# Swin block on one core: who zeroes the values buffers, and where the bias product stands

## What is computed

```python
xn = ln2d(x, norm1_g, norm1_b)                  # over the 64 channels
windows = partition(roll(xn, (-4, -4)), 8)      # 64 windows of 64 tokens
q, k, v = split(windows @ in_w.T + in_b)        # 8 heads of 8 channels
attn = softmax(q @ k.T / sqrt(8)) @ v
y = x + roll(reverse((attn @ out_w.T + out_b) @ proj_w.T + proj_b), (4, 4))
z = ln2d(y, norm2_g, norm2_b)
return y + (gelu(z @ fc1_w.T + fc1_b) @ fc2_w.T + fc2_b)
```

## Time and profile before

| | before |
|---|---|
| median of 3 runs | 90.39 us (90.39 to 90.66) |
| time of the profiled execution | 90.42 us |
| span of the profiled execution | 88.6 us |
| granted TensorE clock, mean | 1.0 |
| busy share: TensorE, VectorE, ScalarE, GpSimd | 93%, 73%, 56%, 47% |

### The profile page before, as it was taken

How to read it: one execution, slowest core, us unless ns; L and a number is a source line. 1 busy time by engine, 2 the same in 40 slices (tenths; PEclk the granted TensorE clock), 3 DMA queues, 4 the chain that set the end, 5 groups by cost and what they waited for, 6 DMA issues and landing times.

```text
span 88.6 us, 4248 instructions
## 1 busy us (share of the span) xinstructions
PE 82.6 (93%) x1794; PEld 51.9 (59%) x1794; DVE 65.0 (73%) x188; ACT 50.1 (56%) x83; POOL 41.7 (47%) x52
## 2 busy tenths in 40 slices
PE   5997999799999999999999999989999999999950
PEld 5974846466775676586686567646664453233420
DVE  4999989898999799669869698999760854333160
ACT  0395998853678296396396156334469486453500
POOL 7988819988108516940930930340717135800000
PEclk9999999999999999999999999999999999999999
DMA  1799400111111111010111110000000000030233
GB/s 23 222 351 424 182 29 0 63 44 52 44 51 37 59 49 51 31 65 31 51 37 59 45 50 24 4 0 11 7 0 7 0 0 0 7 118 37 81 141 100
DMA packets 3619, 5.74 MB, mean 65 GB/s; under 512 B 1072, under 2 KB 1840, under 8 KB 3472
## 3 DMA queue, kind: packets, MB, share of 16 engines
q1 hardware_dynamic: 2736, 3.08, 10.1%
q10 hardware_dynamic: 864, 2.38, 7.1%
HBM read 2.64 MB, written 1.05 MB: 42 GB/s over the span
## 4 chain that ended last, share of the span: by engine, by line
PE 83%; DVE 7%; DMA 3%; issue 2%; ACT 1%; SPq 1%
PE ps_s L310 17%; PE ps_u L392 10%; PE ps_t L375 8%; PE ps_u L467 5%; PE ps_m L285 5%; PE ps_o L408 4%; PE ps_t L310 4%; PE ps_s L451 4%; PE ps_t L451 3%; PE ps_o L420 3%; DMA masked<-qk 3%; PE ps_m L274 2%; PE ps_m L451 2%; PE ps_m L375 2%; PE ps_o L467 2%; PE ps_m L297 2%
## 5 line engine op out<-in xcount | busy, mean ns | idle before, releaser
L883 ACT ACTIVATE probs<-ps_t 128x1024 f32<-128x1024 f32 x13 | 13.3, 1024 | 13.3 <-PE ps_t L375 13.2
L627 DVE TENSOR_REDUCE row_max<-ps_s 128x16 f32<-128x1024 f32 x15 | 18.3, 1219 | 3.1 <-PE ps_s L310 2.4
L310 PE MATMUL ps_s<-masked,qk 32*64 32x256 f32 x240 | 16.8, 387 | 1.1 <-DMA masked<-qk 0.5
L1016 POOL TENSOR_TENSOR rstd<-y_var,minus_half 128x4 f32<-128x4 f32 x8 | 8.2, 1031 | 15.5 <-DVE y_var L681 15.5
L310 PE MATMUL ps_t<-masked,qk 32*64 32x256 f32 x224 | 15.5, 388 | 0.0
L310 PEld LDWEIGHTS ps_s<-masked,qk 32*64 32x64 f32 x240 | 8.4, 131 | 3.9 <-issue 1.4
L392 PE MATMUL ps_u<-probs,vz 128*32 128x64 f32 x512 | 10.5, 222 | 0.0
L392 PEld LDWEIGHTS ps_u<-probs,vz 128*32 128x32 f32 x512 | 7.9, 110 | 4.4 <-issue 4.2
L375 PE MATMUL ps_t<-max_x,minus_sel 128*128 128x512 f32 x26 | 9.4, 443 | 0.0
L992 POOL TENSOR_TENSOR rstd<-var,minus_half 128x4 f32<-128x4 f32 x8 | 8.6, 1070 | 1.0 <-DVE var L615 0.4
L641 DVE STREAM_TRANSPOSE sums<-ps_u 128x512 f32<-128x512 f32 x8 | 5.7, 710 | 4.5 <-PE ps_u L392 4.5
(11 more groups left out here) (110 smaller groups left out, 153.8 us busy)
## 6 DMA issues: line engine op xcount, KB each, us to landing
masked<-qk SPq DMA_DIRECT2D x54, 32.0 KB, 2.1
x_ch<-x_ch_d ACTq DMA_DIRECT2D x1, 1024.0 KB, 8.5
out_d<-result SPq DMA_DIRECT2D x3, 256.0 KB, 2.5
x_tok<-x_tok_d ACTq DMA_DIRECT2D x1, 512.0 KB, 6.4
late<-late_d ACTq DMA_DIRECT2D x1, 352.0 KB, 5.1
x_tok<-x_tok_d SPq DMA_DIRECT2D x2, 128.0 KB, 3.4
x_tok<-x_tok_d ACTq DMA_DIRECT2D x1, 256.0 KB, 4.5
out_d<-result SPq DMA_DIRECT2D x2, 128.0 KB, 2.2
```

Source lines behind the costliest of these rows:

```text
L310: return nc.tensor.matmul(ps[L * u:L * u + L, g, n * TOK:(n + 1) * TOK], qk[r:r + RG, b, w, t], masked[r:r + RG, b, :, w, t], start=(n == ...
L627: nc.vector.tensor_reduce(row_max[:, 16 * w:16 * w + 16], score_bank(k, w)[:].rearrange("q g (h j) -> q (g h) j", j=L), axis=AX.X, op=ALU. ...
L883: nc.scalar.activation(probs[:, w, :], scores_t_bank(k, w)[:].rearrange("q g c -> q (g c)"), ACT.Exp).then_inc(probs_done, 1)
L1016: nc.gpsimd.tensor_tensor(rstd2[:].rearrange("q n w -> q (n w)"), y_var[:].rearrange("q n w -> q (n w)"), minus_half[:], op=ALU.pow).then_ ...
```

## The change

VectorE no longer zeroes `vz` 1. ScalarE zeroes buffer 1 in place of 2 and 3, and GpSimd zeroes 0, 2, 3 and 4. On GpSimd the scaling of tile 2 now waits until VectorE has finished the six masks of tile 0 (`k_masked_dve` at 2), and the scaling of tile 3 until VectorE has masked tile 1 (`k_masked_dve` at 3); `zero_masked(3)`, which waited for the first maxima, now follows the scaling of tile 3. On TensorE the bias product moves from behind the first eight warm-up products to behind `x_transpose(0)`, and of the fourteen warm-up products ahead of the first projection thirteen are left, in another division. The thresholds of the waits for zeroed buffers follow.

```diff
--- before.py
+++ after.py
@@ -137,7 +137,6 @@
         masked_zeroed = [sem(f"masked_zeroed{i}") for i in range(QB)]
         vz_zeroed = sem("vz_zeroed")
         vz_zeroed_act = sem("vz_zeroed_act")
-        vz_zeroed_dve = sem("vz_zeroed_dve")
         vz_set = sem("vz_set")
         bias_product_done = sem("bias_product_done")
         b_qk_made = sem("b_qk_made")
@@ -547,16 +546,16 @@
             pe.wait_ge(zeros_set, 1)
             warm_up(8)
             pe.wait_ge(early_loaded, 16)
-            nc.tensor.matmul(ps_o[:, 0, 0:1], w_in_t[0:C, 0:2 * C], vec[0:C, B1:B1 + 1],
-                             start=True, stop=True).then_inc(bias_product_done, 1)
-            warm_up(3)
+            warm_up(2)
             pe.wait_ge(mean_w_set, 1)
             pe.wait_ge(w_in_scaled, 1)
             nc.tensor.matmul(ps_u[:, 0, 0:3 * C], mean_w[:], w_scaled[:],
                              start=True, stop=True).then_inc(w_in_mean_done, 1)
+            warm_up(2)
+            x_transpose(0)
+            nc.tensor.matmul(ps_o[:, 0, 0:1], w_in_t[0:C, 0:2 * C], vec[0:C, B1:B1 + 1],
+                             start=True, stop=True).then_inc(bias_product_done, 1)
             warm_up(1)
-            x_transpose(0)
-            warm_up(2)
             pe.wait_ge(w_qkv_made, 1)
             project_qk(0)
             late_products_out()
@@ -775,7 +774,7 @@
                     spread_max_dve(t + 1)
                 if t == 0:
                     late_weights()
-                    dve.wait_ge(vz_zeroed, 2)
+                    dve.wait_ge(vz_zeroed, 4)
                     set_ones(VB - 1, VB)
                 if tile_ok(t - 1):
                     scale_attn(t - 1)
@@ -786,7 +785,6 @@
             nc.vector.memset(zeros[:], 0.0).then_inc(zeros_set, 1)
             nc.vector.memset(mean_w[:], 1.0 / P).then_inc(mean_w_set, 1)
             nc.vector.memset(masked[:, 0].rearrange("q h w t -> q (h w t)"), 0.0).then_inc(masked_zeroed[0], 1)
-            nc.vector.memset(vz[:, 1].rearrange("q w n h e -> q (w n h e)"), 0.0).then_inc(vz_zeroed_dve, 1)
             ln1_stats(0)
             ln1_var_first()
             dve.wait_ge(early_loaded, 16)
@@ -812,9 +810,8 @@
             spread_max_dve(0)
             mask_k_half(1)
             ln1_stats(4)
-            dve.wait_ge(vz_zeroed, 1)
-            dve.wait_ge(vz_zeroed_dve, 1)
-            dve.wait_ge(vz_zeroed_act, 2)
+            dve.wait_ge(vz_zeroed, 3)
+            dve.wait_ge(vz_zeroed_act, 1)
             set_ones(0, VB - 1)
             ln1_stats(5)
             for t in range(TILES):
@@ -861,13 +858,11 @@
 
             def copy_v(k):
                 act.wait_ge(v_projected, k + 1)
-                if k in (0, VB - 1):
-                    act.wait_ge(vz_zeroed, 2 if k else 1)
-                elif k == 1:
-                    act.wait_ge(vz_zeroed_dve, 1)
+                if k == 1:
+                    act.wait_ge(vz_zeroed_act, 1)
                 elif k < VB:
-                    act.wait_ge(vz_zeroed_act, k - 1)
-                if k >= VB:
+                    act.wait_ge(vz_zeroed, max(k, 1))
+                else:
                     act.wait_ge(values_weighed, 2 * (k - VB) + 2)
                 for u in range(2):
                     r = slice(L * u, L * u + L)
@@ -940,9 +935,8 @@
             nc.scalar.activation(minus_sel[:].rearrange("q a u j -> q (a u) j"), sel8.unsqueeze(2).to_broadcast([P, 8, L]),
                                  ACT.Copy).then_inc(minus_sel_made, 1)
             act.wait_ge(zeros_set, 1)
-            for b in (2, 3):
-                nc.scalar.activation(vz[:, b].rearrange("q w n h e -> q (w n h e)"), zeros[:, 0:1].to_broadcast([P, 1024]),
-                                     ACT.Copy).then_inc(vz_zeroed_act, 1)
+            nc.scalar.activation(vz[:, 1].rearrange("q w n h e -> q (w n h e)"), zeros[:, 0:1].to_broadcast([P, 1024]),
+                                 ACT.Copy).then_inc(vz_zeroed_act, 1)
             copy_xn(0)
             copy_qk_first()
             mask_k_first()
@@ -1048,16 +1042,18 @@
             ln1_rstd(0)
             ln1_rstd(1)
             ln1_scale(1)
-            pool.wait_ge(early_loaded, 16)
             ln1_rstd(2)
+            pool.wait_ge(k_masked_dve, 2)
             ln1_scale(2)
-            pool.wait_ge(max_found, 1)
+            zero_values(2)
+            zero_values(3)
+            ln1_rstd(3)
+            pool.wait_ge(k_masked_dve, 3)
+            ln1_scale(3)
             zero_masked(3)
-            ln1_rstd(3)
-            ln1_scale(3)
-            zero_values(VB - 1)
             ln1_rstd(4)
             ln1_scale(4)
+            zero_values(4)
             for t in range(TILES):
                 slot(t)
             for k in range(TILES - 3, TILES):
```

## The result

The changed kernel takes 90.84 us, the median of 20 runs; the kernel before takes 90.09 us on the same chip (20 runs). The ratio is 1.0051, with a 95% interval of 1.0029 to 1.0072: slower by some 0.46 us. The profiled execution took 90.77 us with a span of 89.0 us (before: 90.42 and 88.6). One thing has to be known to read the numbers: four of the 20 runs of the changed kernel took 92.7 to 94.3 us at a lower granted clock and are in the median but not in the ratio; the first and the sixth experiment are about them. The other sixteen fall into two groups of eight, at 90.07 to 90.47 us and at 90.77 to 91.19 us, with 90.62 us as the median of all sixteen. The profiled execution is one of the slower group.

A forecast was written before the change was run, and what follows sets the result against it. After the prologue TensorE's products bound the kernel, with VectorE's gapless list holding the hand-over. A later `b_qk` adds 0.33 us, less 0.07 of slack: 90.42 + 0.26 = 90.68 us, range 90.1 to 91.1.

The forecast's parts named there:

- The sum: Whole kernel: +0.33 us on VectorE up to the first maxima, 0.07 taken off in all, giving +0.26 us.
- rival 3: Tile 2: GpSimd, later by its waits, stalls VectorE's masks with the scaling of tile 4; 90.8 to 91.2 us, chance 0.2.
- The base: Start of the forecast: the profiled execution's 90.42 us, taken as 0.03 us above the median of the runs.
- The slack: VectorE between first maxima and tile 1's maxima: idle gaps of 0.19 and 0.07 us; only 0.07 taken off.
- The memset off VectorE: Prologue: without the 0.91 us memset of `vz` 1, `xhat` of tile 0 comes 0.31 us sooner, at 6.38.
- the load of tile 1: VectorE's statistics of tile 1: the load landing at about 5.3 limits the memset's gain to 0.31 to 0.38 us.
- `b_qk`: VectorE, tile 0: waits for the moved bias product, starts at 7.57 to 7.73, taken as +0.33 us, delaying masks and scores.
- rival 1: Tile 0: the early 0.31 us get through if `b_qk` starts before 7.30; 90.1 us, chance 0.13.
- GpSimd's wait for tile 0: Tile 0's masks: the wait removes a 0.37 us stall already covered by the first scores; worth nothing on the path.
- GpSimd's lateness: GpSimd's queued work: costed at nothing; under the slower rival, scaling of tile 4 at about 20.2 meets masks at 20.33.

The follow-up runs named there:

- experiment 1: Changed kernel with the bias product first again, in TensorE's order of before: 90.57 us, ratio 0.9991.
- sixth experiment: Changed kernel with GpSimd's scaling of tile 4 behind VectorE's masks of tile 2, and without two warm-up products before the first projection of v: 94.37 us.
- experiments 4: Kernel before with only the bias product moved behind the transposes of tile 0: 90.77 us, ratio 1.006.
- experiment 2: Changed kernel with GpSimd's scaling of tile 4 also waiting for VectorE's masks of tile 2: 90.45 us, ratio 1.0022.
- experiment 8: Changed kernel, bias product first, tile 4's scaling behind tile 2's masks; also `vz` 0 memset and statistics of tiles 1 and 3 moved later: 90.06 us, ratio 1.0014.
- Experiments 2 and 3: 3 is the changed kernel with both edits, bias product first and tile 4's scaling behind tile 2's masks: 89.81 us, ratio 0.9947; 2 has only the latter.
- experiment 7: Kernel before with GpSimd's scaling of tile 2 waiting for VectorE's six masks of tile 0: 89.97 us, ratio 0.9994.
- execution of 90.05 us: Unchanged changed kernel, one of three further profiles; it is free of the long stall of tile 2's masks: 90.05 us.

## Why the prediction was right

- **The sum.** +0.26 us was forecast, with 90.68 us and ends from +0.07 to +0.43; the ratio gives +0.46 us. The sum describes the executions without the stall: there TensorE's scores of tile 2 are 0.19 us late. In the other half rival 3 came true as well, and they are 0.95 us late. The measured average mixes the two, so it is in part luck that it lies near the sum.
- **The base.** 90.42 us was the time of one execution, which loses 0.4 us at 50 us, and the median of 20 runs is 90.09. From there the sum gives 90.35 us, against 90.62 measured at full clock. The 90.68 us came close because the base was 0.33 us too high and the stall was not in the sum.
- **The slack.** 0.07 us was taken off between the first maxima and those of tile 1. The delay shrank there from 0.38 us (11.95 against 11.57) to 0.21 (19.03 against 18.82): 0.17 us.
- **The memset off VectorE.** `xhat` was put at 6.38 and came at 6.44, and the -0.31 is -0.34 to -0.41 between experiments 4 and 2, within the noise. The reason was only half right. It was not the load of tile 1: VectorE waited for tile 0's own load until 3.73, and for GpSimd's power for the last 0.20 us. And the variance (L614) took 0.42 us, ending at 5.21 where GpSimd's memset of `vz` 0 ended at 5.19; without that memset beside it, it took 0.17 (experiment 8), as it did before, behind the memset's end.
- **`b_qk`** was put at 7.57 to 7.73 and came at 7.70; the idle gap before it, put at 0.6, was 0.57. Masks at 9.76 (9.84), first scores at 10.75 (10.79), first maxima at 11.9 (11.95), maxima of tile 1 at 19.1 (19.03): the line of work was the right one. Experiments 2 and 3 show that `b_qk` has little slack (of 0.67 us some 0.5 get through), and rival 1 was right in its condition: with `b_qk` at 7.04 the early 0.25 us get through.
- **GpSimd's wait for tile 0.** Costed at nothing, and experiment 7 gives a ratio of 0.9994.
- **GpSimd's lateness.** Scaling of tile 4 at about 20.2 and masks at 20.33 were forecast, 20.34 and 20.27 came. The step that was mis-sized is the price of their meeting: "by the fifth mask of tile 0 this costs 0.37 us, and at most the whole 0.62". The scaling cost 0.35 us, as the row said, and was swallowed, but behind it on GpSimd stood a memset of 0.95 us, which the change had moved there from behind the scaling of tile 3, and the mask waited for that too: 1.24 us in all (2.13 against 0.89). And rival 3 counted slack where there is none: it let the maxima at 21.33 be late against the scores at 26.07, but TensorE's scores at 22.78 follow them with 0.22 us between, so what is left after the 0.38 us of idle time reaches TensorE at once. I had looked for what stands behind the waiting instruction on its own engine, and not for what stands behind the one that holds it up.
- The rule of the Trainium skill that I set beside it (SBUF — State Buffer, Who interferes with whom: the pair of ports is an exclusive lock for a whole instruction, and the other fully blocks) agrees in kind with the rows: the second of the masks that took 2.13 us together ended only after the scaling and the memset had, and in the execution of 90.05 us the memset waited for the mask. That a waiting instruction is passed over for a second one of the other engine is more than that rule says.

## What to carry to other kernels

When a product or a load is moved, look at who reads it in whose order: a bias of one column, two microseconds early before, cost about 0.5 us once it stood behind a wait, because all of an engine's list stood behind its reader. When two engines that block each other are brought to within a tenth of a microsecond of each other, price the collision with everything that is queued behind the holder, and expect it to come out one way or the other from run to run; a wait that settles the order (experiment 2) costs nothing where the held instruction has slack. A single profiled execution is a weak base for a forecast of 0.3 us: compare its time with the median of many runs first. And work that only fills time, such as warm-up products, must be recounted whenever a hole moves.

## What the runs showed of the hardware that was not expected

- A waiting instruction can lose twice: in two of four profiled executions of the changed kernel a mask on VectorE was held by GpSimd's scaling and then by the memset issued behind it, 1.2 us in all, though the mask stood waiting before the memset was issued.
- A GpSimd memset, which reads nothing, holds up a VectorE TENSOR_SCALAR with one input in fp32: a variance of 128x4 took 0.42 us beside it (0.68 in experiment 1, where it started sooner) and 0.17 without it.
- Idle times of TensorE of 0.39 and 0.69 us, a microsecond apart, were followed in the profiled execution by half clock until about 25 us, and five of six runs took 94 us or more; with one gap of 0.51 us, 6 of 56 runs were at 94 us.
- One gap of 0.74 us behind the stall of tile 2 was followed by half clock from 24 to 27 us in experiment 1's profiled execution; gaps of 0.69 and 0.72 us at the same place were not, in the two of the changed kernel.
- TensorE can lose 0.4 to 0.5 us inside a group of products for which neither the program nor the profile has a wait; it did so at 50 us in three of ten profiled executions at full clock.
